# A third early tile for expert 1, and the bias rows of experts 1 to 7 loaded two tiles sooner

## What is computed

```python
h = _layernorm(x) * (1 + cb) + sb
gate_scores = softmax(h @ Wg + bg)
topk_scores, topk_idx = top_k(gate_scores, 2)
topk_scores = topk_scores / (sum(topk_scores) + 1e-08)
for e in range(8):                       # W1[e]: 256 x 1024, W2[e]: 1024 x 256
    y = gelu(h @ W1[e] + b1[e]) @ W2[e] + b2[e]
    output = output + y * combine_w[..., e:e + 1]
x = x + gb * output
```

## Time and profile before

| | |
|---|---|
| median of 3 runs | 750.69 us (750.62 to 750.79) |
| the profiled execution | 751.8 us, of which the span from first to last instruction 749.9 |
| PE busy | 702.4 us (94% of the span), 4856 matmuls |
| PEld busy | 646.1 us (86%) |
| DVE busy | 503.3 us (67%) |
| ACT busy | 419.9 us (56%) |
| POOL busy | 400.5 us (53%) |
| mean granted clock of PE | 0.978 of full |
| DMA | 72.77 MB, mean 97 GB/s |

### The profile page before, as it was taken

The page is one execution under the profiler, slowest core; times in us unless marked ns, Lnnn a source line. Parts: engine busy times, 40 slices in busy tenths (PEclk is TensorE's granted clock), DMA queues, the critical chain, the costliest instruction groups (busy, mean ns, idle before and its releaser), DMA issues.

```text
span 749.9 us, 16194 instructions
## 1 busy us (share of the span) xinstructions
PE 702.4 (94%) x4856; PEld 646.1 (86%) x4856; DVE 503.3 (67%) x1751; ACT 419.9 (56%) x1058; POOL 400.5 (53%) x317
## 2 busy tenths in 40 slices
PE   5799999999999999998799999999999999999992
PEld 2578888788888888896699999999999999999992
DVE  5869879997878785774654574556866565466451
ACT  4556556556564645655444665656666576475561
POOL 1165536786765665455753464446555365473443
PEclk9799999999999998999989999999999999999997
DMA  8371011212204223253633534565653555433433
GB/s 302 95 240 51 8 57 65 93 33 82 87 8 140 81 73 115 84 140 77 156 73 57 125 66 69 124 134 167 153 98 65 130 125 120 80 60 64 70 70 47
DMA packets 50603, 72.77 MB, mean 97 GB/s; under 512 B 5968, under 2 KB 42396, under 8 KB 50528
## 3 DMA queue, kind: packets, MB, share of 16 engines
q0 software_dynamic: 16480, 27.28, 19.5%
q1 hardware_dynamic: 34048, 44.60, 19.2%
HBM read 48.85 MB, written 23.01 MB: 96 GB/s over the span
## 4 chain that ended last, share of the span: by engine, by line
PE 75%; DVE 8%; issue 6%; DMA 5%; ACT 2%; POOL 2%; another core or an unknown queue 1%; SPq 1%; DVEq 0%; POOLq 0%; ACTq 0%
PE yb L1078 22%; PE mm L1068 22%; PE mm L973 19%; PE yb L998 6%; PE tp L1059 2%; DMA out_x<-ysb,tokb 1%; PE tp L1032 1%; DMA gbr<-mod_rows,xm 1%; PE tp L988 1%; DMA x2b<-in_L_ffn_b 1%; DVE ytmp L1520 1%; DMA h2all<-in_L_wmod 1%; DMA mb<-mod_rows 1%; PE tp L1009 1%
## 5 line engine op out<-in xcount | busy, mean ns | idle before, releaser
L905 ACT ACTIVATE hh<-mm,vT 128x256 fp32r<-128x256 f32 (+1 forms) x288 | 135.5, 471 | 162.9 <-PE mm L1068 114.2
L658 POOL DMA_INDIRECT out_x<-ysb,tokb x68 | 110.7, 1628 | 187.6 <-DVE ysb L1528 149.7
L1499 DVE TENSOR_TENSOR hl<-mm,hh 128x256 fp32r<-128x256 f32 (+1 forms) x288 | 116.3, 406 | 123.1 <-ACT mm L906 95.7
L1068 PE MATMUL mm<-fh,SH 128*128 128x256 f32 x576 | 165.8, 288 | 15.4 <-DVE hl L1499 10.5
L1068 PE MATMUL mm<-fl,SH 128*128 128x256 f32 x576 | 162.3, 282 | 0.2 <-issue 0.2
L1068 PE MATMUL mm<-fh,SL 128*128 128x256 f32 x576 | 162.3, 282 | 0.0
L1078 PE MATMUL yb<-SH,hh 128*128 128x256 f32 x544 | 157.4, 289 | 2.1 <-issue 1.1
L1078 PE MATMUL yb<-SL,hh 128*128 128x256 f32 x544 | 153.8, 283 | 1.1 <-issue 1.1
L1078 PE MATMUL yb<-SH,hl 128*128 128x256 f32 x544 | 153.6, 282 | 0.0
L1068 PEld LDWEIGHTS mm<-fh,SH 128*128 128x128 f32 x576 | 110.3, 192 | 19.3 <-DVE hl L1499 12.5
L906 ACT ACTIVATE mm<-mm,vT 128x256 f32<-128x256 f32 (+1 forms) x288 | 126.8, 440 | 0.0
(11 more groups left out here) (226 smaller groups left out, 1162.0 us busy)
## 6 DMA issues: line engine op xcount, KB each, us to landing
xin<-disp_x SPq DMA_DIRECT2D x74, 132.0 KB
wraw<-in_L_ffn_W SPq DMA_DIRECT2D x8, 1024.0 KB
h2all<-in_L_ffn_W SPq DMA_DIRECT2D x8, 1024.0 KB
xb<-in_L_attn_x SPq DMA_DIRECT2D x8, 512.0 KB, 7.0
out_x<-x2b SPq DMA_DIRECT2D x8, 512.0 KB
mb<-mod_rows SPq DMA_DIRECT2D x3, 768.0 KB, 6.4
wraw<-in_L_attn_W_ugg SPq DMA_DIRECT2D x1, 1536.0 KB, 12.1
gbr<-mod_rows,xm POOLq DMA_INDIRECT x74
```

The lines of the kernel that those rows point to most:

```text
L658: e.indirect_dma_start(out=out_rows, out_offset=bass.IndirectOffsetOnAxis(ap=tokb[:, j:j + 1], axis=0), in_=ysb[:, j, :], in_offset=None, ...
L905: e.activation(hh[:, f, c_], mm[f % 4][:, c_], ACT.Gelu_apprx_tanh, bias=bias)
L1068: i = e.matmul(mm[f % 4][:, 0:TE], a[:, k, f * 128:(f + 1) * 128], b[:, k, :], start=(k == 0 and t == 0), stop=(k == 1 and t == 2))
L1499: e.tensor_tensor(hl[:, f, w_], mm[f % 4][:, w_], hh[:, f, w_].bitcast(F32), ALU.subtract)\
```

## The change

Three things change together.

1. NE becomes 8: there are three early tiles of expert 1 instead of two (tiles 5, 6 and 7), in the programs of all five engines. POOL's bursts stay where they are, one ahead of each of tiles 2 to 5.
2. The counts follow: `bounds` has a tenth column, which holds min(768, rows of expert 1 in groups 0 to 5) where the ninth held min(512, those rows). The late tiles of expert 1 begin at the tenth.
3. SP issues the load of the bias rows, with its three waits, right behind the row load of tile 4.

```diff
-NE0, NE = 5, 7
+NE0, NE = 5, 8
...
-        bounds = sb(ctx, "bounds", [128, 9])
+        bounds = sb(ctx, "bounds", [128, 10])
...
                 if i == 3:
                     load_w2(2)
+                if i == 4:
+                    e.wait_ge(S["x2_scaled"], NG)
+                    e.wait_ge(S["x2_stored0"], 16 * (NG // 2))
+                    e.wait_ge(S["x2_stored1"], 16 * (NG // 2))
+                    e.dma_start(b2b[:, 1:E, :].rearrange("p e d -> p (e d)"),
+                                b2[1:E, :].rearrange("e d -> (e d)").partition_broadcast(128)).then_inc(S["b2_loaded1"], 16)
             e.reg_alu(r_pos, r_pos, r_end, ALU.min)
             e.reg_add(r_late[1], r_pos, -CAP)
             e.reg_mov(r_pos, r_late[0])
 
-            e.wait_ge(S["x2_scaled"], NG)
-            e.wait_ge(S["x2_stored0"], 16 * (NG // 2))
-            e.wait_ge(S["x2_stored1"], 16 * (NG // 2))
-            e.dma_start(b2b[:, 1:E, :].rearrange("p e d -> p (e d)"),
-                        b2[1:E, :].rearrange("e d -> (e d)").partition_broadcast(128)).then_inc(S["b2_loaded1"], 16)
...
-                    e.tensor_scalar(bounds[:, 7:9], fills[:, 0:2], base[:, 1, 1:2], float(CAP), ALU.min, ALU.add)
+                    e.tensor_scalar(bounds[:, 7:10], fills, base[:, 1, 1:2], float(CAP), ALU.min, ALU.add)
...
-                yield from lk(e, e.tensor_scalar(less[:, 1:2], bounds[:, 8:9], float(CAP), None, ALU.subtract), "dve_a")
+                yield from lk(e, e.tensor_scalar(less[:, 1:2], bounds[:, 9:10], float(CAP), None, ALU.subtract), "dve_a")
...
-                    mark(e.tensor_tensor(nom[:, :], nom0, bounds[:, 8:9].to_broadcast([128, 2]), ALU.add))
+                    mark(e.tensor_tensor(nom[:, :], nom0, bounds[:, 9:10].to_broadcast([128, 2]), ALU.add))
```

## The result

The changed kernel takes 746.99 us (median of 5 runs, 745.78 to 747.42) against 750.79 (5 runs, 750.62 to 753.1) of the kernel before on the same chip: ratio 0.9938, 95% interval 0.9921 to 0.9955. That is 1.6 us above the forecast of 745.4 and inside its own range of 743.7 to 747.8. The profiled execution took 747.06 us, span 745.0, against 751.8 and 749.9.

What follows compares the result with a forecast made beforehand. PE bounds the kernel with 75% of the span, but in tile 5 waits through DVE for the bias load. 751.8 - 7.98 + 1.2 + 1.0 + 0.5 = 746.5, from the median 745.4; own range 743.7 to 747.8, overall 741.8 to 750.0.

Steps and rivals of the forecast that it cites:

- The wait for the bias load and its half clock, -7.98: Tile 5: with the load issued at 336.8, DVE's 5.5 us wait and the clock's fall go, -7.98 us.
- the rival whose clock falls in tile 3: Tile 3: the bias load stretches PE's idle from 1.82 to 5.57 us and the clock falls; 755.6 us, chance 6%.
- The late gelu, +1.2: Tile 5: ACT's late first gelu frees the buffer at 369.85, PE wants it at 368.70; +1.2 us, bounds 0 and 1.2.
- the sends at full speed, +1.0: Tile 5 and start of tile 6: the last burst of sends meets PE at full speed; +1.0 us, bounds 0 and 3.60.
- the sign of 13 to 16 us: Sign that the forecast holds: tile 5 lasts 13 to 16 us, not 19.93.
- the second rival: Tile 5: the sends take the wait's place and it becomes like tile 3, 18.67 us; 749.9 us in all, chance 12%.
- The granted clock stays 1.00 from 366 to 386.: Sign that the forecast holds: no fall of the clock in that span, around tile 5.
- The bias load beside tile 3: Tile 3: 896 KB loaded beside a scatter may delay the second burst by 2 us; +0.5 us, bounds -1.8 and +1.9.
- The moved tile: Expert 1: one full tile goes from late (11.98 us) to early (11.95), the count stays 36; 0, bounds -0.03 and +0.03.
- SP reads the counts after sends have landed; they get 12 us more for that: Seam between early and late tiles: it comes one tile later, giving sends 12 us more to land; no gain counted.
- POOL without the stall: Tile 5: burst 375 to 380, scatter at 380.4, gathers landed by 389, DVE reads at 389.3; within the 0 to 3.6.
- The sum: Whole kernel: all terms together give -5.3 us, 745.4 us from the median; chance 53%.

Runs made afterwards that it cites:

- load_at_5: Changed kernel with the bias load one tile later, behind the row load of tile 5: 731.26 us, ratio 0.9934 to the kernel before.
- load_only: Changed kernel with two early tiles of expert 1 instead of three, so only the bias load is moved: 731.85 us, ratio 0.993 to the kernel before.
- load_at_5_again: Changed kernel with the bias load behind the row load of tile 5, run beside the changed kernel on one chip: 729.62 us, ratio 0.9901.
- the burst divided: Changed kernel with its last burst of four sends split, two beside tile 5 and two beside tile 6: 742.61 us, ratio 0.9904.
- load_only_burst_early: load_only with both of the last bursts of four sends beside tile 4: 749.35 us, ratio 0.9994 to the kernel before.
- the burst moved: Changed kernel with its last burst of four sends beside tile 6 instead of tile 5: 730.71 us, ratio 0.9926; on another chip 742.43 us.
- burst_extra: Changed kernel with the last burst issued a second time beside tile 6, SP waiting for it before the late rows: 732.2 us, ratio 0.9931.

## Why the prediction was right, and where it was not

- *The wait for the bias load and its half clock, -7.98.* Right. The wait is gone in every kernel with the load moved, and where nothing takes its place all of the excess goes (6.99 of 18.89 on a prompt chip). That it is the load and not the third tile is shown by the two halves: 0.993 and 1.0008. The term is the 5.73 us that PE lost, and the half clock behind it: by the earlier trace rows 24 matmuls took 5.60 us at the clock of 0.50, and 49 took the next 5.60 at 1.00. At 5.60 / 49 = 0.114 us each 24 take 2.7 us; they took 5.2 (5.60 less the 0.43 before the first), so 2.4 more, an estimate from these rows. 5.7 + 2.4 = 8.1, against 7.98 between tiles 5 and 6. The price of the rival whose clock falls in tile 3 has the same 2.4; its fall did not come: the clock of tile 3 is 1.00 in both profiles of the changed kernel on late chips.
- *The late gelu, +1.2, and the sends at full speed, +1.0 with bounds 0 to 3.6.* Here the sum mis-sized both terms. It put tile 5 at 19.93 - 7.98 + 1.2 + 1.0 = 14.15 us; it came out as 18.31, outside the sign of 13 to 16 us. The gelu was as late as read, but DVE started another 0.45 us behind it (366.63, where ACT had ended at 366.18): PE lost 1.99 us where 1.2 had been put. The half clock behind that wait, some 1.4 us, had been put at nothing. Of the excess over a plain tile, 18.31 - 11.95 = 6.36, some 3.0 are left for the sends and other late signals (by subtraction). On the late chip of the experiments the burst alone costs 3.58, the upper bound, and without it 1.49 are left for the rest (1.2 forecast). Nearness to 0 had been chosen because tile 5 has none of the splits and the place chain of tile 3; they were not what made tile 3 long, since on prompt chips it has them too and lasts 11.94. And the upper bound was itself too low: it counted the idle time of tile 3, 3.60, but its 15.07 us of busy PE were stretched as well, against 11.94 on a prompt chip; all that tile 3 lost was 18.67 - 11.94 = 6.73. By its stretch, tile 5 of the result is the second rival (18.67), not the forecast.
- *"The granted clock stays 1.00 from 366 to 386."* Wrong: 0.50 from 368 to 370. The remark that an idle of 1.82 us left the clock at 1.00 did not carry: one of 1.83 with slow gelus behind it did not leave it there, nor did one of 1.77 in tile 19 of load_at_5 (0.50 from 523 to 525). An idle of 2.22 in load_only did (1.00 from 374 to 382). The length of the idle alone does not tell.
- *The bias load beside tile 3, +0.5.* Tile 3 shrank by 2.20 us instead, beyond the bound of -1.8. On prompt chips it is 11.94 with the load and 11.95 without, so the load costs nothing there. On late chips five profiles with the load there give 14.72 to 16.47, but only one without it, 18.67. Whether the load's place or chance did it stays open.
- *The moved tile, 0.* Right: 11.94 for tile 7, 36 tiles (x576 of L1069), and the tile with the seam lasts 13.23 against 13.20. But "SP reads the counts after sends have landed; they get 12 us more for that" was put at nothing. That is right only while tile 5 is long. Once it is short, load_only's tile 6 shows what those 12 us hide, 2.43 us in its profile. By the profiles, then, the two halves of the change are worth more together than apart; the medians do not resolve it.
- *POOL without the stall.* "It fits by a hair" was too cautious. The burst began at 371.45, not 375, and POOL then stood idle for 5.76 us before the scatter of tile 5, waiting for DVE.
- *The sum.* Tile 5 lies 4.2 us over the forecast, tile 3 2.7 under it, tile 6 0.4 under it (11.54), and the stage of the groups, which no part of the change explains, 1.5 under; what follows the early stage is 0.7 over. These nearly cancel. That is luck: the total was right by more than its reasoning earned. The fall was 0.6% on the chip of the result and 0.9% on a prompt one; the single run on the other late profile's chip, 743.75 against 750.28, is 0.9% too.

No version tried beats the changed kernel beyond the intervals: load_at_5_again 0.9901 beside 0.9909, and the burst divided 0.9904 on a chip where the changed kernel had a single time.

## What to carry to other kernels

When a wait on a load and the low clock behind it go, ask what else that long stretch was hiding: here the sends for the late rows needed a whole tile between themselves and their reader (with one between them tile 7 is 11.95 us; without, PE's tile is 1.1 to 2.4 us longer), so the tile that gave nothing alone was worth 2.4 us in the profiles. Price a burst of indirect writes at full engine speed by all that the stretch that has one lost against a plain one, busy time too (6.73 us in tile 3), and not from a discounted share of its idle time (3.60 there). And where two edits are made together, time each alone and both: their gains need not add.

## What the runs showed of the hardware

- The kernel before takes 736 us on two chips and 750 on the late ones. Of the 15.5 us between the spans of before on a late and a prompt chip (749.9 and 734.4), 13.25 lie in its seven early tiles (114.02 and 100.77 us): 6.7 in tile 3, 4.8 in tile 0, in whose first half eight sends run, 1.1 in tile 1 and 1.0 in tile 5. On the late ones ACT and DVE start work late without a named cause ("remote", or a PE that had long been done); the row "ACT hh <- remote" of the waits (11.6 us in the kernel before, 15.5 and 12.2 in the two profiles of the changed one) is missing on the prompt ones. In one profile, that of load_only_burst_early, PE itself starts matmuls 0.72 us apart marked "issue". This comes with bursts of sends beside tiles 3 and 5 but not beside tile 6 (11.95 with the burst moved, 11.53 with it divided), at a DMA share of 0.48 in tile 5 against 0.57 on a prompt chip, where nothing is late. What the signals wait for was not found.
- In burst_extra a prompt chip had such lateness in two tiles too, and load_at_5's profile had one in tile 19 (15.46 us, clock 0.89). So it is not wholly a matter of the chip. Nor is it known whether the chip of the result and the late one of the experiments are two.
- Most sends, gathers and scatters hold POOL for the same time on both: 0.96 to 1.01 us for a send or a gather, 1.6 to 1.8 for a scatter.
